# Turning 13 steps of an FFN's second product in the first token pass, with w1 split ahead during attention

## The reference

```
x = x + tanh(g_xattn) * (softmax(q k^T / 8) v Wo + bo)     # q from layernorm(x), k and v from ctx (8, 750, 512), 8 heads of 64
f = layernorm(x)
for each expert e of 8:                                    # every token goes through every expert
    h = gelu(f w1[e] + b1[e])                              # w1: 512 x 1024
    y = y + h w2[e] + b2[e]                                # w2: 1024 x 512
x = x + tanh(g_ffn) * norm_g * y                           # norm_g: a factor for each token from a small gating network
```

## Time and profile before

| | us |
|---|---|
| median of 3 runs | 1806.14 |
| lowest, highest | 1804.5, 1806.62 |
| the profiled execution, its own time | 1805.74 |
| its span, first to last instruction | 1803.9 |
| busy in the span: TensorE / VectorE / ScalarE / GpSimd | 1774.5 / 1393.2 / 920.4 / 1230.9 |

### The profile page before, as it was taken

The page is one execution under the profiler, slowest core; times in us unless marked ns, Lnnn a source line. Parts: engine busy times, 40 slices in busy tenths (PEclk is TensorE's granted clock), DMA queues, the critical chain, the costliest instruction groups (busy, mean ns, idle before and its releaser), DMA issues.

```text
span 1803.9 us, 34041 instructions
## 1 busy us (share of the span) xinstructions
PE 1774.5 (98%) x9752; PEld 1619.3 (90%) x9752; DVE 1393.2 (77%) x2389; ACT 920.4 (51%) x1793; POOL 1230.9 (68%) x1049
## 2 busy tenths in 40 slices
PE   7999999999999999999999999999999999999998
PEld 7999999999999878888888888888899999999987
DVE  7888878888887875656565656569998998989987
ACT  6767676677666843333333333344444444444443
POOL 5525455263544768777677767849988989889863
PEclk9999999999999999999999999999999999999999
DMA  5111102021120246353535353535343343343432
GB/s 175 42 32 46 50 25 58 22 70 41 34 69 10 77 179 253 131 192 128 192 128 192 128 192 128 192 142 185 124 147 131 132 156 118 144 152 121 146 105 94
DMA packets 56671, 211.06 MB, mean 117 GB/s; under 512 B 13721, under 2 KB 26009, under 8 KB 48417
## 3 DMA queue, kind: packets, MB, share of 16 engines
q1 hardware_dynamic: 56608, 210.30, 33.4%
HBM read 140.55 MB, written 69.73 MB: 117 GB/s over the span
## 4 chain that ended last, share of the span: by engine, by line
PE 94%; DVE 3%; issue 1%; ACT 1%; DMA 0%; SPq 0%; POOL 0%; ACTq 0%; DVEq 0%
PE scores L894 28%; PE bank L753 20%; PE bank L922 17%; PE bank L951 13%; PE scores L824 5%; PE bank L834 5%; PE bank L846 4%; DVE acc_t L1356 1%; PE bank L760 1%; PE scores L1045 0%; DVE hs L1128 0%; DMA ctx_raw<-in_ctx 0%; PE bank L894 0%; PE bank L987 0%; DVE h_diff L1330 0%
## 5 line engine op out<-in xcount | busy, mean ns | idle before, releaser
L894 PE MATMUL scores<-xs,w1s 128*128 128x448 f32 x2646 | 572.3, 366 | 6.4 <-ACT h_sum L1525 4.6
L894 PEld LDWEIGHTS scores<-xs,w1s 128*128 128x128 f32 x2646 | 494.3, 188 | 56.2 <-ACT h_sum L1525 10.2
L922 PE MATMUL bank<-w2s,hs 128*128 128x512 f32 x1344 | 315.7, 390 | 1.1 <-DVE xres L1246 1.1
L922 PEld LDWEIGHTS bank<-w2s,hs 128*128 128x128 f32 x1344 | 252.1, 188 | 51.5 <-issue 1.5
L1525 ACT ACTIVATE h_sum<-scores 128x448 f32<-128x448 f32 x189 | 102.0, 540 | 353.5 <-PE scores L894 353.5
L1356 DVE TENSOR_TENSOR acc_t<-bank,acc_t 128x448 f32<-128x448 f32 x426 | 246.9, 614 | 18.8 <-PE bank L951 18.7
L1128 DVE TENSOR_TENSOR hs<-h_full,hs 128x448 fp32r<-128x448 f32 x130 | 146.5, 1127 | 99.0 <-ACT hs L1684 97.3
L1286 DVE TENSOR_TENSOR h_sum<-scores,h_sum 128x448 f32<-128x448 f32 x189 | 117.5, 622 | 107.4 <-PE scores L894 81.8
L1788 POOL TENSOR_SCALAR probs<-probs,row_inv 112x750 f32<-112x750 f32 x60 | 130.6, 2177 | 100.1 <-DVE row_inv L1217 100.1
L1301 DVE TENSOR_TENSOR acc<-bank,acc 128x512 f32<-128x512 f32 x217 | 144.3, 683 | 44.1 <-PE bank L922 43.0
L1683 ACT ACTIVATE h_full<-h_sum,b1T 128x448 f32<-128x448 f32 x162 | 108.1, 667 | 127.9 <-DVE h_sum L1286 101.6
(11 more groups left out here) (169 smaller groups left out, 3324.5 us busy)
## 6 DMA issues: line engine op xcount, KB each, us to landing
w_scratch<-w1s SPq DMA_DIRECT2D x32, 1792.0 KB, 7.9
w1s<-w_scratch SPq DMA_DIRECT2D x32, 1792.0 KB, 7.3
w_stage<-in_L_ffn_w SPq DMA_DIRECT2D x96, 512.0 KB, 4.3
ctx_raw<-in_ctx SPq DMA_DIRECT2D x16, 376.0 KB, 3.2
ctx_raw<-in_ctx SPq DMA_DIRECT2D x14, 374.0 KB, 3.2
xa<-in_x SPq DMA_DIRECT2D x16, 224.0 KB, 2.8
xres<-in_x SPq DMA_DIRECT2D x16, 224.0 KB, 2.7
x_scratch<-xres SPq DMA_DIRECT2D x16, 224.0 KB, 2.3
```

What stands on the lines that cost most here:

```text
L894: mm = pe.matmul(product_bank(g, name)[:, 0:TH], w1s[j % 2][:, s, W_OF[name], kc, :], xs[:, i, m, kc, :], start=opens and n == 0, stop=n == 5,
L922: mm = pe.matmul(bank[:, :], hs[j % 2][:, s, ht, t * P:(t + 1) * P], w2s[j % 2][:, m, ht, :], start=n == 0, stop=n == 5)
```

## The change

Thirteen steps of the first pass take the turned form: j = 3 of expert 0 and j = 1 and 3 of experts 1 to 6. The other 19 stay plain. VectorE, ScalarE and GpSimd follow the form of each step: sums and sums_t are merged, a plain step behind a turned one makes its lows h_low between the additions of the turned one. acc_t is set to zero by GpSimd in step (0,0,1), gathers the turned steps of the first pass, and is transposed onto the seven tiles of that pass's last step by 28 transposes more (turn_onto). The column form of b2 is made at step (0,0,1) instead of (1,0,0); the load of x for the second pass moves from (0,0,1) to (0,7,0), and GpSimd's mixing of it from j = 0, 1 to j = 1, 2 of expert 7, since that memory is now in use.

The w1 operands of these 13 steps and of (0,7,1), 14 blocks, are made during attention instead of in the FFN, in halves (one of the two 128-row slices c of a block): four halves a batch, E0 to E3 in GpSimd's plan, in batches 0 to 6. A half is loaded by SP into the space of w2_stage (256 KB in runs of 512 bytes), split by GpSimd (split_ahead, eight instructions of half the size of w1_part's) into the space of w2s0, and stored by SP (896 KB in runs of 512 bytes). There is one space for raw data and one for the result: a load waits for the split before it, a split's first copy for the store before it. In the FFN these 14 steps reload their w1 block (1792 KB) two steps ahead. The w1 split of a plain step is made two steps ahead, in the plain step before it.

The diff, cut to its core:

```diff
+ROWS, TURNED = 19, 13
+AHEAD = 4
...
     "pool": plan("""
-        D<7 M1.1 L<1.0 L<1.1 M2.1 D1 M3.1 C>0.0 C>0.1 L>0.0 L>0.1 M4.1 D3 M5.1 C>1.0 C>1.1 M6.1 D5 M7.1 M>0.1
+        D<7 M1.1 E0 L<1.0 E1 L<1.1 M2.1 D1 M3.1 C>0.0 C>0.1 L>0.0 L>0.1 M4.1 D3 M5.1 C>1.0 C>1.1 M6.1 E2 D5 M7.1
+        E3 M>0.1
     """),
...
+        ahead_raw = w2_stage[:, :, :].rearrange("p a n -> p (a n)").rearrange("p (k n) -> p k n", k=8)
+        ahead_out = w2s[0][:, :, :, :].rearrange("p a b n -> p (a b n)")[:, 0:2 * NM * P].rearrange(
+            "p (s m n) -> p s m n", s=2, m=NM)
...
+        def turned(g):
+
+            p, e, j = g
+            if p or not isinstance(e, int):
+                return bool(p) or j % 2 == 1
+            return e != NE - 1 and j == 3 if e in (0, NE - 1) else j % 2 == 1
+
+        def stored_ahead(g):
+
+            return g[0] == 0 and (turned(g) or at(g, (0, NE - 1, 1)))
...
+            def load_ahead(b, k):
+
+                e, j, c = ahead_place(b, k)
+                if not (isinstance(b, int) and b == 0 and k == 0):
+                    sp.wait_ge(ahead_split, b * (2 * AHEAD) + 2 * k)
+                    alone(sp, passed["sp"])
+                sp.dma_start(ahead_raw[:, 0:4, :], w1[e, j][:, :, c, :]).then_inc(ahead_loaded, 16)
+
+            def store_ahead(b, k):
+
+                e, j, c = ahead_place(b, k)
+                sp.wait_ge(ahead_split, b * (2 * AHEAD) + (2 * k + 2))
+                alone(sp, passed["sp"])
+                sp.dma_start(w1_scratch[e, j].rearrange("p (k c n) -> p k c n", c=2, n=P)[:, :, c, :],
+                             ahead_out[:, :, :, :].rearrange("p s m n -> p (s m) n").bitcast(F32)
+                             ).then_inc(ahead_stored, 16)
...
             def batch(name, plan, b):
+                if name != "last":
+                    load_ctx(b + 1, 0)
+                if name != "first":
+                    store_ahead(b - 1, 2)
+                    load_ahead(b - 1, 3)
+                    store_ahead(b - 1, 3)
                 if name == "last":
                     load_w2((0, 0, 0))
-                if name != "last":
-                    load_ctx(b + 1, 0)
+                else:
+                    load_ahead(b, 0)
                 if name == "first":
                     sp.wait_ge(pool_w_lo, len(POOL_PIECES))
                     for qt in range(2):
                         load_xres(b, qt)
                 else:
                     store_x2(b - 1, 0)
+                if name != "last":
+                    store_ahead(b, 0)
+                    load_ahead(b, 1)
+                if name != "first":
                     store_x2(b - 1, 1)
                     load_xres_next(b)
+                if name != "last":
+                    store_ahead(b, 1)
+                    load_ahead(b, 2)
...
-                if then and then[0] == 1:
+                if then and (then[0] == 1 or stored_ahead(then)):
                     reload_w1(then)
+                if at(g, (0, NE - 1, 0)):
+                    sp.wait_ge(z_psum, NZ * TURNED)
+                    load_x_raw(1)
...
+            def turn_onto(bank, t):
+
+                for d in range(KC):
+                    tr = pe.matmul(bank[:, d * P:(d + 1) * P], acc_t[d][:, t * P:(t + 1) * P], ident[:, :],
+                                   start=d == 0, stop=d == KC - 1, is_transpose=True, skip_group_check=True)
+                return tr
...
+                onto = at(g, (0, NE - 1, JS - 1))
+                if onto:
+                    turn_onto(bank, t)
...
+            def split_ahead(b, k):
+
+                raw, w = ahead_raw, ahead_out
+                begin = isinstance(b, int) and b == 0 and k == 0
...
+                pool.wait_ge(ahead_loaded, b * (16 * AHEAD) + 16 * (k + 1))
+                alone(pool, passed["pool"])
+                pool.tensor_tensor(raw[:, 4], raw[:, 0], raw[:, 3], ALU.add).then_inc(ahead_step, 1)
+                pool.tensor_tensor(raw[:, 6], raw[:, 1], raw[:, 0], ALU.subtract).then_inc(ahead_step, 1)
+                if not begin:
+                    pool.wait_ge(ahead_stored, b * (16 * AHEAD) + 16 * k)
+                    alone(pool, passed["pool"])
+                pool.tensor_copy(w[:, 0, 0:3], raw[:, 1:4]).then_inc(ahead_step, 1)
...
+                pool.tensor_tensor(w[:, 1, 3:7], raw[:, 4:8], w[:, 0, 3:7].bitcast(F32),
+                                   ALU.subtract).then_inc(ahead_split, 1)
...
                 elif not at(g, (0, 0, 0)):
                     split_w2(g)
+                    ahead = not at(g, (0, NE - 1, 1)) and not at(g, (0, NE - 1, 3))
+                    if ahead:
+                        w1_part(then, 0)
+                        if turned(after):
+                            add_w2(after)
+                        for k in range(1, 5):
+                            w1_part(then, k)
                 if at(g, (0, 0, 1)):
+                    pool.wait_ge(in_psum["Y"], B * 2)
+                    for d in range(KC):
+                        pool.memset(acc_t[d][:, :], 0.0).then_inc(acc_zeroed, 1)
```

More of the change, by code:

```diff
@@ new lines, in row_bank, with back, slot_free @@
+        def row_bank(g, t):
+            p, e, j = g
+            shift = 3 * j if isinstance(e, int) and e == 0 else 0
+            return ps[(shift + t) % RING]
+        def back(g, n):
+            p, e, j = g
+            j -= n
+            if isinstance(e, int) and j < 0:
+                e, j = e - 1, j + JS
+                if e < 0:
+                    return (p - 1, NE - 1, j) if p else None
+            return p, e, j
+        def slot_free(eng, g):
+            user = back(g, 2)
+            if user is None:
+                return
+            if turned(user):
+                eng.wait_ge(z_psum, since_turn(NZ, user, NZ))
@@ L498, in previous @@
         def previous(g):
[L499 to L502, removed]
+            return back(g, 1)
         def following(g):
@@ L711, in step @@
                 then = after and following(after)
-                if then and then[0] == 0:
+                if then and then[0] == 0 and not stored_ahead(then):
                     load_w1(then)
-                if after and after[0] == 0:
+                if after and after[0] == 0 and not stored_ahead(after):
                     store_w1(after)
@@ L968, in turn_y @@
                     pe.wait_ge(h_act, upto(4, END, 3))
-                for d in range(KC):
-                    tr = pe.matmul(end_bank(t)[:, d * P:(d + 1) * P], acc_t[d][:, t * P:(t + 1) * P], ident[:, :],
-                                   start=d == 0, stop=d == KC - 1, is_transpose=True, skip_group_check=True)
+                tr = turn_onto(end_bank(t), t)
                 tr.then_inc(end_turned, 1)
@@ L1058, in step @@
                 before = previous(g)
-                turned = before[0] == 1
                 if turns(g):
@@ L1071, in step @@
                         gate(p, i // 2)
-                    if turned:
+                    if turned(before):
                         for k in z_after(g, i):
@@ L1078, in step @@
                         second(before, 0)
-                if turned:
+                if at(g, (0, 0, 1)):
+                    turn_b2()
+                if turned(before):
                     for k in z_rest(g):
@@ L1740, in step @@
                     hidden(g, i)
-                    if p and i == 0 and not at(g, TURN):
+                    if i == 0 and turned(previous(g)):
                         if at(g, AFTER_TURN):
@@ L1755, in step @@
                                        scale=1.0 / TEMPERATURE).then_inc(gate_exp, 1)
-                if p and not at(g, END) and not at(g, TURN):
+                if turned(g) and not at(g, END) and not at(g, TURN):
                     for name in ("T1", "T3", "T2"):
@@ L2018, in step @@
                                        ALU.pow).then_inc(gate_pow, 1)
-                after = following(g)
-                if after and after[0] == 0 and not at(g, (0, 0, 0)):
-                    for k in range(5):
-                        w1_part(after, k)
                 if at(g, (1, 0, 0)):
@@ L2027, in step @@
                                            ALU.subtract).then_inc(x_split_pool, 1)
+                after = following(g)
+                then = after and following(after)
                 if at(g, END):
```

277 lines of the change are left out of this document (171 added, 106 removed).

## The result

The changed kernel takes 1831.26 us (median of 4 runs, 1830.35 to 1833.22) against 1805.32 us of the kernel before, measured beside it: a ratio of 1.0146, 95% interval 1.0128 to 1.0164. It is slower, by 25.9 us; the forecast was 1818 us, slower by 12. The profiled execution has a span of 1829.6 us against 1803.9.

The account below looks back on a forecast made before the run. TensorE, busy 98% of the span, was taken to bound the kernel. Terms -11.7, +3.3, +1, +9.4, +9.0 and +1 sum to +12.0 us, forecasting 1818 us; eight in ten from 1799 to 1838.

Parts of the forecast that it names:

- 13 turned steps: First pass: h times w2 with 448 instead of 512 columns saves 0.89 us a step, -11.7 us.
- 28 transposes: Last step of the first pass: four transposes of acc_t for each of seven tiles on TensorE, +3.3 us.
- late additions on VectorE: Plain steps behind turned ones: additions that matmuls into the same bank wait for, +1 us, bounds 0 and 6.5.
- batch 0, wait: Attention, first batch: TensorE waits for a scaling behind two splits standing together, +9.0 us.
- batch 0, clock: Attention, first batch: TensorE's slow start after that wait, +1 us, range 0 to 2.1.
- batches 1 to 6: Attention: E1 ends 1.6 us late in each of six batches, +9.4 us.
- the prediction's own sign: First pass: the prediction is wrong if turned steps take as long as plain ones; about 17.2 us expected.
- E: Attention: time of one GpSimd split of half a w1 block, taken as 6.0 us, bounds 4.6 and 10.2.
- G: Attention: time from one split's end to the next one's data, taken as 6.0 us, bounds 2.9 and 7.5.
- E1 is on time: Rival in attention: 512-byte runs move at 326 GB/s, G = 4.6, batches 1 to 6 undelayed: 1807 us, chance 0.18.
- faster: Rival in attention: splits take 4.6 to 5 us, loads don't queue, only batch 0 late: 1802 us, chance 0.17.
- dearer: Rival in attention: E = 6.4 and G = 6.6, 30 us lost over six batches: 1840 us, chance 0.13.

Follow-up runs that it names:

- The two cures: Two runs on the changed kernel: VectorE's two late subtractions put behind the additions, 1815.94 us; GpSimd's w1 split part held until VectorE's subtractions are made, 1816.0 us.
- the late subtractions: The changed kernel with VectorE's subtractions for h blocks 2 and 3 behind the last of its 14 additions into acc_t: 1815.94 us, ratio 1.006.
- the feed-forward part alone: The changed kernel without GpSimd's w1 splits during attention and the 28 loads for them, the 28 stores kept: 1812.63 us, ratio 1.0048.
- the second split in two parts: The changed kernel with each batch's second split cut in two around the scaling of head 3, its store and load issued later: 1817.69 us, ratio 1.0065.
- the load ahead of the store: The changed kernel with SP issuing the next raw block's load before the store of the block just split: 1824.15 us, ratio 1.0099.
- GpSimd held: The changed kernel with GpSimd's third w1 split part held until VectorE made that step's four subtractions: 1816.0 us, ratio 1.0053.
- the second split moved: The changed kernel with each batch's whole second split behind the scaling of head 4, its store and load issued later: 1847.9 us, ratio 1.0229.

## Why the prediction was right in its direction and wrong in its size

| term of the sum | forecast, us | measured, us | from |
|---|---|---|---|
| 13 turned steps | -11.7 | -12.6 | 432.96 - 421.36 for 12, times 13/12 |
| 28 transposes | +3.3 | +2.5 | 7 tiles, 0.36 from their start to the first matmul's |
| late additions on VectorE | +1 (0 to 6.5) | +17.9 | 437.90 - 421.36 for 12, times 13/12 |
| batch 0, wait | +9.0 | +8.7 | the wait of line 942 |
| batch 0, clock | +1 (0 to 2.1) | +2.0 | the same matmuls behind the wait: 70.34 - 64.25 against 58.90 - 54.81 |
| batch 0, the rest | none | +0.8 | 123.17 - 111.67 less these two; 0.55 of it stood before the wait |
| batches 1 to 6 | +9.4 | +8.4 | six periods, 597.84 - 123.17 against 577.98 - 111.67 |
| last batch, no split in it | none | -1.6 | 671.03 - 597.84 against 652.73 - 577.98 |
| first tile of the pass's last step | none | +2.4 | the wait of line 1013 |
| turn into the second pass | 0 | about -2 | the 2.16 us at 1249.25 before |

They add up to 26.5 us; the spans differ by 25.7. (The first term should have read 13 x 0.888 = 11.5 by its own rows, which changes nothing.) The two cures gave back only 15.3 us of the 17.9 by their medians. The traces show a part of the difference: in both of them the clock fell behind the 2.4 us wait of the pass's last step, and from its transposes to the next product that step took 8.9 us in place of 7.35, 1.6 us that the changed kernel had not paid; and holding GpSimd left one place of the 13 as it was.

**The step that failed** is the VectorE term: "What could be late is an addition that the next matmuls into the same bank wait for. Bounds 0 and 13 x 0.5 = 6.5 us (I see no gain in it); I take +1, near zero because the late work is at the end of the step." It measured 17.9 us, and by the prediction's own sign (turned steps that take as long as the plain ones) it was wrong: a pair took 36.49 us for 36.08. The place was named rightly, the price wrongly, for two reasons that the two cures keep apart. The end of the step is just where the last product waits for the 9th addition, so nothing there is hidden by what comes later; a count of VectorE's work over two steps couldn't show that. And the subtractions were priced at their mean of 1.13 us, while the 130 of the kernel before run from 0.61 to 2.61 us, with a median of 0.90 and 28 of them over 2.1: 0.61 us alone, 2.2 us in the place shown, beside GpSimd's long subtraction. With 0.61 the term would have been nothing, as in the run that holds GpSimd, and even 1.13 us would have let the addition end at about 926.2, as TensorE came free (an estimate from the rows of that place); with 2.2 it is 1 us in each of 13 steps. The wait then cost 1.38 us a pair, not the 1.06 that the row of waits shows. A group of six matmuls is 1.38 us long but the next one starts 1.22 us behind its start, and the row counts from the end: at the place shown the start moved by 2.41 - 1.22 = 1.19 us, and the group that waited took 1.33 us to the next start, 0.11 more.

**What held.** The gain of the form: 0.97 us a step where the 25 steps of the second pass gave 0.89. Batch 0: 9.0 against 8.7. E: 5.4 us, below the 6.0 taken and inside its bounds. G: 6.3 to 7.1 us against 6.0, so that E0, the gap and E1 were 17.3 us in the batch shown for 18.0, and a batch lost 1.4 us for 1.6. The place of every wait in attention came as described, though the waits of batches 1 to 6 were mostly shorter than the 1 to 3 us of the forecast. So "E1 is on time" fell on the traffic, as weighed, "faster" on the traffic and the price of E, and "dearer" on the price of E. That the clock would fall behind batch 0's wait was right; the price was the upper bound and not the half that I took.

The rule of the Trainium skill, "DMA: Bandwidth & Descriptors", section "Anatomy of one DMA", would have made G 4.7 us; the measured 6.3 to 7.1 decides against it here, for runs of 512 bytes behind a store in the same queue. That section states its figures for DMAs that GpSimd issues; SP issues these, so the prediction used them outside of what they are given for. The other one, "TensorE: Matmul & The Clock Gate", Part 1, made the slow start 2.1 us instead of 1: 2.0 were measured, so it was right and my half was not.

**What was missed altogether:** the wait of 2.4 us in the pass's last step. A tile's wait was written there for all additions of the step before, which costs nothing where 30 matmuls of the next step stand between, and in that step none do. It was in the code to be read.

## What to carry to other kernels

A duration that is a mean over one kind of instruction should be split into its shortest and longest before it prices a new place: different neighbourhoods hide in it. Where work is put between additions that free a bank, ask for each one which matmul waits for it and when, not whether the step has room. Idle time on an engine with a fixed order counts in the pieces in which it comes: the same split moved whole (5.4 us) made the kernel 16.6 us slower, and moved in two parts 13.6 us faster.

## What the hardware showed that was not expected

TensorE's clock does not fall alike after waits of one length. After batch 0's wait of 8.7 us in the changed kernel it read 0.50 for at least 3.8 us, and the matmuls there took 2.0 us more than in the kernel before, as the table has it:

```profile
64.20:66.00 1.80, 1.75 (x7) 1.76 (x8) 0.00 (x0) 0.54 (x1) 0.89 (x2) 0.50 1.00 262
66.00:68.00 2.00, 2.00 (x10) 1.98 (x9) 1.56 (x2) 0.50 (x1) 0.00 (x0) 0.50 0.98 249
```

After 2.4 us in attention it fell as well, in all seven batches of the run that moved E1, to between 0.50 and 0.67 in stretches of 2 to 3 us behind the wait. After the same 2.4 us in the last step of the first pass it stayed at 1.00 in the changed kernel and was 0.57 in the run with the late subtractions. Seven runs have that wait, and behind it the clock stayed at 1.00 in four of them (the changed kernel, the feed-forward part alone, the second split in two parts, the load ahead of the store) and fell in three (the late subtractions, GpSimd held, the second split moved). The stretch behind the wait in the changed kernel and with the late subtractions:

```profile
1246.80:1249.00 2.20, 2.14 (x13) 1.85 (x14) 2.17 (x2) 0.00 (x0) 2.20 (x2) 1.00 0.00 0
```

```profile
1227.70:1230.00 2.30, 2.21 (x8) 1.95 (x9) 2.12 (x1) 0.00 (x0) 2.30 (x2) 0.57 0.00 0
```

The 12 waits of about 1.06 us in the 438 us above left the mean clock of that stretch at 1.00. Yet in the last batch of attention of the kernel before it fell behind waits of 1.19 and 0.98 us:

```profile
626.80:633.60 6.80, 6.80 (x23) 5.66 (x22) 5.42 (x9) 5.85 (x11) 3.84 (x4) 0.50 0.38 108
```

The changed kernel's execution has no such fall there, and from the matmuls at 626.18 (646.06 in it) to the next output projection it is 1.5 us shorter: that is the -1.6 of the table, a difference between two executions and no gain of the change. What decides was not tried and stays open; for a forecast, a wait of 2.4 us can cost 1.6 to 2 us on top of its length, or nothing.

The price of sharing between VectorE and GpSimd was larger than a mean shows: 2.23 us for a subtraction of 0.61. It fell on VectorE, which came second; GpSimd's subtraction took 1.86 us in both runs.
